# Expert weights split ahead through a DRAM scratch, the last scores first, token halves alternating

## The chip, the cores and the metric

The kernel runs on one core of a Trainium2 chip. A core has five engines with queues of their own: TensorE (PE) multiplies, VectorE (DVE) and ScalarE (ACT) work element by element, GpSimd (POOL) computes a little and issues indirect DMAs, and SyncE (SP) only issues DMAs. They meet at semaphores. The metric is the time of one execution on the device, in microseconds; the median of the runs shown is quoted, and one further execution is profiled.

## The reference, cut to what matters

N = 4096 tokens, D = 512 features, E = 8 experts.

```python
# graph attention, with a residual
q = layernorm(x) @ Wq.T + bq;  k = key @ Wk.T + bk;  v = value @ Wv.T + bv
s = (q @ k.T) / 64 * adj
s = where(abs(s) < 1e-5, -1e9, s)
x = x + (softmax(s) @ v) @ Wm.T + bm
# mixture of experts, two of eight, with a residual
xn   = layernorm(x)
gate = softmax(xn @ Wg + bg);  the top 2 kept and scaled to sum 1
x    = x + sum_e gate_e * (xn @ We[e].T + be[e])
```

## The kernel before

Every large product is made of half-precision parts: an operand is split into a high half (f16) and what is left of it (f16), and three matmuls are summed, high·high, high·low, low·high. `product` does it.

**Folding and projection (until 239 us).** The weights of q and k are folded into one matrix, and those of v and the output projection into another. Keys, values and q are brought into that form by groups of 512 tokens. Keys and values stay in SBUF (`key_region`, `val_region`); q goes to a DRAM scratch, `q_scratch`.

**Attention (32 tiles of 128 query rows; `attend` on each engine, `attend_io` on SyncE).** A tile has 8 chunks of 512 keys. TensorE makes the scores of a chunk (`scores`, 12 matmuls of 128x512) and, one tile behind, the product of a chunk of probabilities with the values (`times_values`, also 12). VectorE multiplies scores with the adjacency (`times_adj`, L967), masks them and finds maxima (`mask`, L974 and L977), ScalarE takes magnitudes (`absolute`, L737) and exponentials (`exponent`, L745 and L750), VectorE splits these (`low_half`, L989), and SyncE turns them with DMA transposes (`turn_probs`, L474). Two tiles behind, the finished rows are normalised and routed: top 2 of 8 experts (`route_top2`), the gates (`route_gates`, for which ScalarE computes one exponential, `gap_exponent`, L784), and the slot that each row gets in its expert's region (`route_slots`, L1089). GpSimd then scatters the rows with two indirect DMAs (`scatter_row`) into a DRAM table `slots`, one table for each half of the tokens. The inverse deviation of the rows (`inverse_deviation`, L618) stands behind these scatters in GpSimd's queue. The single buffer of q, `q_in`, is reloaded at a tile's end (L503), behind the adjacency loads (L465).

Every engine works off its own instructions in the order written. The order within a tile is written out by hand in `attend` and `attend_io`.

**Experts (78 blocks of 128 slots, 39 for each half).** When all rows of a half are in their regions, `tables` computes which rows and which expert each block has. For each block SyncE loads 128 token rows (`load_block`, L547), TensorE turns them (`turn_block`, L1430) and multiplies them with the expert's weights (`multiply_block`, 12 matmuls), ScalarE and VectorE split the turned rows (`block_hi`, `block_lo`), VectorE adds the bias (`block_bias`, L1240), ScalarE applies the gate (`block_gate`, L822), and GpSimd adds the rows to the output with an indirect DMA (`add_block`, L662). If an expert's first block comes up, the accumulations before it must have landed, since the same token may be in both. TensorE turns blocks two ahead of the one that it multiplies. The rest of a region's last block is filled with rows of zero weight (`pad_regions`, 8 DMAs of which each reads its address from a table).

The raw expert weights are loaded in 1 MB pieces over the keys' space and next to it once the last scores are done (L527, L532, L796); ScalarE and VectorE split them, half an expert at a time (`expert_hi`, L798; `expert_lo`, L1197), the first eight halves beside the last tile's probabilities and the other eight between the first eight blocks. Blocks of the first half all come before those of the second.

Of the kernel before, what the change touches and what calls it, by code (L numbers as in the profile page):

```python
# [6 lines left out]
F16 = mybir.dt.float16  # L7
# [12 lines left out]
def graph_attention_moe_kernel(nc, x, adj, keyT, valueT, Wq, bq, Wk, bk, Wv, bv, WmT, bm, Wg, bg, WeT, be, outs):  # L20
# [37 lines left out]
    EARLY = 23  # L58
    LATE = 7
# [8 lines left out]
    assert TURN % RING == 0 and (BLOCKS - EARLY) % TURN == 0 and (BLOCKS - LATE) % TURN == 0 and (T % HALVES) == 0  # L68

    SPLIT_EARLY = C  # L70
    assert SPLIT_EARLY == E and 2 * E - SPLIT_EARLY <= EARLY
# [7 lines left out]
    with ctx:  # L79
# [15 lines left out]
        we = key_region[:, :].rearrange("p (h e k o) -> p h e k o", h=2, e=E, k=KC)  # L95
# [43 lines left out]
        q_in1 = q1_words.bitcast(F16).rearrange("p (h k n) -> p h k n", h=2, k=KC)  # L139
        behind = q1_words[0:1, 0:BLOCKS * E].rearrange("p (b e) -> p b e", b=BLOCKS)  # L140
# [4 lines left out]
        we_odd = carve(KC * D).rearrange("p (k o) -> p k o", k=KC)  # L145
        tokT = carve(YB * KC * P).bitcast(F16).rearrange("p (b h k n) -> p b h k n", b=YB, h=2, k=KC)
        we_even = carve(KC * D).rearrange("p (k o) -> p k o", k=KC)
        we_in = (we_even, we_odd)
# [6 lines left out]
        tok_in += [moe_words[:, at:at + ROW] for at in range(RING * D, RING * D + (RING - YB) * ROW, ROW)]  # L155
        assert len(tok_in) == RING and 12288 + YB * ROW <= 14848
# [73 lines left out]
        o_bank = ps[:, 4, :]  # L230

# [15 lines left out]
        weT_v = WeT.rearrange("e (k p) o -> e p k o", p=P)  # L247
# [61 lines left out]
        we_loaded = [sem(f"we_loaded{b}") for b in range(2)]  # L309
        we_hi = sem("we_hi")  # L310
        we_lo = sem("we_lo")
        be_loaded = sem("be_loaded")
# [24 lines left out]
        tok_loaded = [sem(f"tok_loaded{b}") for b in range(RING)]  # L337
# [9 lines left out]
        halves_of_k = (slice(0, KC // 2), slice(KC // 2, KC))  # L347
# [3 lines left out]
        class Step:  # L351


            def __init__(self, first, turn, h):
                self.first, self.turn, self.h = first, turn, h
                self.at = first + turn * TURN if not is0(turn) else first
                self.b2, self.bank, self.b8, self.meta = first % 2, first % YB, first % RING, first % TURN
# [13 lines left out]
            def has(self, back):  # L371
                return self.first >= back

        def early_steps():
            return [Step(s, 0, 0) for s in range(EARLY)]

        def late_steps():
            return [Step(BLOCKS + s, 0, 1) for s in range(LATE)]

        def turn_steps(j, h):  # L380

            return [Step((EARLY, BLOCKS + LATE)[h] + i, j, h) for i in range(TURN)]

        TURNS = ((BLOCKS - EARLY) // TURN, (BLOCKS - LATE) // TURN)

        AHEAD = 2
        MIDDLE = (SEQ - EARLY) // TURN

        def middle_steps(j):

            return [Step(EARLY + i, j, None) for i in range(TURN)]

        def end_steps():
            return [Step(s, 0, None) for s in range(EARLY + MIDDLE * TURN, SEQ)]

        def ahead(st):

            return Step(st.first + AHEAD, st.turn, None)
# [4 lines left out]
        def _(sp):  # L403
# [77 lines left out]

            def attend_io(t, h=None, last=False):

                turn_probs(t - 1, 0)
# [20 lines left out]
            def pad_regions(h):  # L505
# [997 lines left out]
```

## Time and profile before

| | us |
|---|---|
| median of 3 runs | 1904.28 (1902.39 to 1905.7) |
| the profiled execution | 1899.79 |
| its span, first to last instruction | 1898.1 |
| TensorE busy | 1817.8 (96%) |
| VectorE, ScalarE, GpSimd busy | 1176.2, 730.1, 239.4 |
| granted clock of TensorE, mean | 0.981 of full speed |

The page's row of slices has TensorE at 9 tenths or more until slice 33 of 40, and holes in slices 34 to 37. A row of the stages view gives, for a stretch in us from the span's start, its length, then for PE, PEld (weight loads), DVE, ACT and POOL the busy time with the number of instructions in brackets, and at the end the granted clock, the busy share of the 16 DMA engines, and GB/s. A row of a timeline gives start, duration, engine, line, operation, output and inputs, and in square brackets how long the engine had been idle before it and for what. SPq and ACTq are the issues of DMAs; the duration there is that of the issue. The chain of waits is the chain of work that ended last, with start and duration of each link.

### The profile page before, as it was taken

The numbers are of one execution on the slowest core, as the hardware profiler recorded it, in microseconds if no ns is written. First come the engines' busy times: TensorE is split into PE (matmuls) and PEld (weight loads), VectorE is DVE, ScalarE is ACT, GpSimd is POOL, SyncE is SP. The second block draws the span as 40 slices with busy tenths as digits, with TensorE's granted clock in tenths as the row PEclk, the third lists the DMA queues.
The fourth block names the chain that finished last, engine by engine and source line by source line (L and its number), as shares of the span: only waits on it lengthen the run. The fifth ranks groups of instructions, "written<-read, shape, count | busy, mean of one in ns | idle before, by whom it ended". The sixth has DMA issues, their size and how long they took to land.

```text
span 1898.1 us, 32739 instructions
## 1 busy us (share of the span) xinstructions
PE 1817.8 (96%) x8730; PEld 851.0 (45%) x8731; DVE 1176.2 (62%) x3056; ACT 730.1 (38%) x1381; POOL 239.4 (13%) x277
## 2 busy tenths in 40 slices
PE   8999999999999999999999999999999996789994
PEld 4544444444444444444444444444444443345552
DVE  2788766666666666666666666666666664634542
ACT  1444444443333344433333344433333442433341
POOL 1000000100000000000000000000000010444454
PEclk9999999999999999999999999999999998899997
DMA  5355455555555555555556555555555558788785
GB/s 200 111 177 188 172 136 124 140 142 137 139 138 133 133 133 145 137 142 134 139 128 176 135 135 144 134 145 133 138 133 136 134 137 244 180 194 165 162 161 78
DMA packets 410860, 279.67 MB, mean 147 GB/s; under 512 B 316737, under 2 KB 316737, under 8 KB 410690
## 3 DMA queue, kind: packets, MB, share of 16 engines
q1 hardware_dynamic: 390914, 234.55, 47.8%
q0 software_dynamic: 16736, 38.35, 10.2%
q10 hardware_dynamic: 3168, 6.29, 1.0%
q8 instruction: 16, 0.26, 0.1%
q14 instruction: 26, 0.21, 0.0%
HBM read 144.29 MB, written 59.33 MB: 107 GB/s over the span
## 4 chain that ended last, share of the span: by engine, by line
PE 75%; DVE 8%; DMA 7%; issue 5%; SPq 2%; ACT 2%; DVEq 0%; POOLq 0%; POOL 0%; ACTq 0%
PE ps L1280 16%; PE ps L1282 16%; PE ps L1281 16%; PE ps L1380 8%; PE ps L1381 8%; PE ps L1382 8%; DMA work<-q_scratch 4%; DVE work L967 2%; PE ps L1289 2%; PE ps L1430 1%; ACT work L737 1%; DMA work<-in_WeT 1%; DMA work<-work 1%; PE ps L1327 1%; DVE work L974 1%
## 5 line engine op out<-in xcount | busy, mean ns | idle before, releaser
L1280 PE MATMUL ps<-key_region,work 128*128 128x512 f16 (+1 forms) x1336 | 509.9, 382 | 9.8 <-DMA work<-q_scratch 7.0
L1281 PE MATMUL ps<-key_region,work 128*128 128x512 f16 (+1 forms) x1336 | 509.4, 381 | 0.0
L1282 PE MATMUL ps<-key_region,work 128*128 128x512 f16 (+1 forms) x1336 | 509.2, 381 | 0.0
L1380 PE MATMUL ps<-val_region,work 128*128 128x512 f16 x1024 | 389.6, 380 | 16.3 <-DMA work<-work 11.4
L737 ACT ACTIVATE work<-work 128x512 f32<-128x512 f32 x256 | 161.3, 630 | 597.2 <-DVE work L967 597.1
L1382 PE MATMUL ps<-val_region,work 128*128 128x512 f16 x1024 | 389.6, 380 | 0.0
L1381 PE MATMUL ps<-val_region,work 128*128 128x512 f16 x1024 | 389.5, 380 | 0.0
L967 DVE SCALAR_TENSOR_TENSOR work<-ps,r_cur,work 128x512 f32<-128x512 f32 x256 | 191.8, 749 | 179.0 <-PE ps L1282 163.3
L989 DVE TENSOR_TENSOR work<-work 128x512 f16<-128x512 f32 x256 | 176.4, 689 | 84.0 <-ACT work L750 83.1
L977 DVE CUSTOM_DVE_ANT_0 work<-work 128x512 f32<-128x512 f32 x256 | 177.3, 693 | 51.2 <-DVE work L974 51.0
L1280 PEld LDWEIGHTS ps<-key_region,work 128*128 128x128 f16 x1336 | 131.2, 98 | 172.9 <-issue 28.8
L745 ACT ACTIVATE work<-work,exp_bias 128x512 f32<-128x512 f32 x256 | 181.4, 708 | 65.6 <-DVE exp_bias L985 61.5
L1282 PEld LDWEIGHTS ps<-key_region,work 128*128 128x128 f16 x1336 | 131.4, 98 | 158.8 <-issue 3.4
L1281 PEld LDWEIGHTS ps<-key_region,work 128*128 128x128 f16 x1336 | 131.3, 98 | 148.0 <-issue 3.0
L750 ACT ACTIVATE work<-work,exp_bias 128x512 f16<-128x512 f32 x256 | 180.7, 706 | 0.0
L974 DVE TENSOR_SCALAR work<-work 128x512 f32<-128x512 f32 x256 | 109.2, 426 | 113.2 <-ACT work L737 109.2
L1380 PEld LDWEIGHTS ps<-val_region,work 128*128 128x128 f16 x1024 | 100.2, 98 | 131.8 <-DMA work<-work 12.0
L1382 PEld LDWEIGHTS ps<-val_region,work 128*128 128x128 f16 x1024 | 100.4, 98 | 122.0 <-issue 1.9
L1381 PEld LDWEIGHTS ps<-val_region,work 128*128 128x128 f16 x1024 | 100.4, 98 | 114.0 <-issue 1.5
L662 POOL DMA_INDIRECT out<-val_region,tok_ids x78 | 123.9, 1588 | 152.7 <-DMA out<-val_region,tok_ids 66.6
L627 POOL COPY work<-gate 128x1 f32<-128x1 f32 x64 | 14.6, 228 | 856.9 <-DVE slots_u L1089 776.6
L822 ACT ACTIVATE val_region<-work,tok_gates 128x512 f32<-128x512 f32 x78 | 56.3, 722 | 160.6 <-DVE work L1240 138.8
(149 smaller groups left out, 1542.9 us busy)
## 6 DMA issues: line engine op xcount, KB each, us to landing
work<-in_adj SPq DMA_DIRECT2D x256, 256.0 KB, 2.8
work<-slots SPq DMA_DIRECT2D x40, 257.0 KB
val_region<-slots SPq DMA_DIRECT2D x38, 257.0 KB
work<-in_valueT SPq DMA_DIRECT2D x8, 1024.0 KB, 6.8
work<-in_x SPq DMA_DIRECT2D x8, 1024.0 KB, 5.0
work<-in_keyT SPq DMA_DIRECT2D x8, 1024.0 KB, 5.4
q_scratch<-work SPq DMA_DIRECT2D x8, 1024.0 KB, 5.0
work<-q_scratch SPq DMA_DIRECT2D x32, 256.0 KB, 3.0
```

Of the source, the lines that this page charges most:

```text
L737: nc.scalar.activation(w[:, c * CW:(c + 1) * CW], s_adj[:, c % 2, :], ACT.Abs).then_inc(abs_done, 1)
L745: nc.scalar.activation(prob[:, c % 2, :], w[:, c * CW:(c + 1) * CW], ACT.Exp, bias=exp_bias[:, :], scale=1.0 / SS, accum_out=sum_part[:, c ...
L750: nc.scalar.activation(p_split[:, c, 0:CW], w[:, c * CW:(c + 1) * CW], ACT.Exp, bias=exp_bias[:, :], scale=1.0 / SS).then_inc(p_hi, 1)
L967: nc.vector.scalar_tensor_tensor(s_adj[:, c % 2, :], s_bank(c), r_cur[:, :], adj_in[:, c % ADJ, :], ALU.add, ALU.mult).then_inc(s_read, 1)
L977: nc.vector.tensor_tensor_reduce(out=masked, in0=s_adj[:, c % 2, :], in1=masked, scale=1.0, scalar=-3.0e38, op0=ALU.add, op1=ALU.max, accu ...
L989: nc.vector.tensor_tensor(p_split[:, c, CW:2 * CW], prob[:, c % 2, :], p_split[:, c, 0:CW], ALU.subtract).then_inc(p_lo, 1)
L1280: nc.tensor.matmul(bank, st[0], mv[0], start=(k == 0), stop=False)
L1281: nc.tensor.matmul(bank, st[0], mv[1], start=False, stop=False)
L1282: last = nc.tensor.matmul(bank, st[1], mv[0], start=False, stop=(k == n - 1))
L1380: nc.tensor.matmul(o_bank, st[0], mv[0], start=first, stop=False)
L1381: nc.tensor.matmul(o_bank, st[0], mv[1], start=False, stop=False)
L1382: last = nc.tensor.matmul(o_bank, st[1], mv[0], start=False, stop=final)
```

## The change

Weights. In attention tiles 2 to 17 (the first half), each half of an expert is loaded in four pieces of 256 columns, split by ScalarE and VectorE, and stored as f16 halves in a DRAM scratch, `we_halves`. After the last scores ScalarE issues the loads of expert 0 from the scratch; those of experts 1 to 7, with each expert's bias row, once the last probabilities have been turned. SyncE passes their arrival on through one semaphore, `we_ready`. The splitting at the end is gone.

Last tile. TensorE makes the scores of the last tile before most of the value products of the tile before (`attend_last`). The last tile's values are summed in another PSUM bank.

Blocks. 15 blocks of the first half lead, then 48 blocks alternate between the halves, then 15 of the second half are the tail. Token buffers are 16 instead of 8. The second half's padding is issued by ScalarE after block 9; its last rows are scattered behind accumulations 6 and 8.

```diff
-    EARLY = 23
-    LATE = 7
+    LEAD = 15
+    TOKS = 16
+    PIECES = 4
+    WP = D // 2
+        we_stage = q1_words[:, 0:WP]
+        we_halves = q1_words[:, WP:2 * WP].bitcast(F16).rearrange("p (h o) -> p h o", h=2)
+        o_last = ps[:, 3, :]
+        weT_parts = WeT.rearrange("e (a k p) (c o) -> (e a) p k c o", a=2, p=P, c=2)
+        we_dram = nc.dram_tensor("we_halves", (2 * E, P, 2, 2 * D), F16, kind="Internal").ap()
...
 # SyncE
+            def split_piece(i, q):
+                if not (is0(i) and q == 0):
+                    sp.wait_ge(piece_lo, i * PIECES + q)
+                settle()
+                sp.dma_start(we_stage, weT_parts[i, :, q // 2, q % 2, :]).then_inc(piece_loaded, 16)
+            def store_piece(i, q):
+                sp.wait_ge(piece_lo, i * PIECES + q + 1)
+                settle()
+                sp.dma_start(we_dram[i, :, :, q * WP:(q + 1) * WP], we_halves).then_inc(piece_stored, 16)
             def attend_io(t, h=None, last=False):
+                splits = h == 0
+                if splits:
+                    split_piece(t - 2, 0)
                 turn_probs(t - 1, 0)
...
                 turn_probs(t - 1, 3)
+                if splits:
+                    store_piece(t - 2, 0)
+                    split_piece(t - 2, 1)
                 if h is not None:
                     residual_io(t - 2, h)
                 adjacency(t, 7)
                 for c in range(ADJ, C):
                     turn_probs(t - 1, c)
                     if not last:
                         adjacency(t + 1, c - ADJ)
                     if c == 4 and h is not None:
                         turn_rows(t - 2)
+                    if splits and c in (5, 6, 7):
+                        store_piece(t - 2, c - 4)
+                        if c < 7:
+                            split_piece(t - 2, c - 3)
                 if not last:
                     sp.wait_ge(s_mm, t * C + C)
                     settle()
                     sp.dma_start(q_in, q_dram[t + 1]).then_inc(q_loaded, 16)
...
+            def expert_ready(e):
+                sp.wait_ge(we_loaded[e], 48)
+                sp.sem_inc(we_ready, 1)
+            for st in lead[:YB]:
                 load_block(st)
+            expert_ready(0)
+            sp.wait_ge(pv_mm, T * C)
+            load_block(lead[4])
+            load_block(lead[5])
+            sp.wait_ge(x1_done, T)
+            sp.dma_start(out_tiles[1][TH - 1], x1_out).then_inc(x1_stored, 16)
+            expert_ready(1)
+            turn_rows(T - 1)
+            for st in lead[6:]:
+                load_block(st)
+            for e in range(2, E):
+                expert_ready(e)
+            sp.wait_ge(slotted, 32 * T)
+            sp.wait_ge(padded[1], 16 * E)
+            (48 blocks of turn_steps, 15 of tail_steps)
...
 # ScalarE
+            def piece_high(i, q):
+                act.wait_ge(piece_loaded, i * (PIECES * 16) + (q + 1) * 16)
+                if not (is0(i) and q == 0):
+                    act.wait_ge(piece_stored, i * (PIECES * 16) + q * 16)
+                nc.scalar.activation(we_halves[:, 0, :], we_stage, ACT.Copy, scale=WS).then_inc(piece_hi, 1)
                 for c in range(2, 4):
                     absolute(t, c)
+                    if splits:
+                        piece_high(t - 2, c - 2)
                 if routes:
                     split_rows(t - 2)
                 for c in range(4, 7):
                     absolute(t, c)
+                    if splits and c > 4:
+                        piece_high(t - 2, c - 3)
                 if routes:
                     gap_exponent(t - 2)
                 absolute(t, 7)
...
+            act.wait_ge(piece_stored, 16 * PIECES * 2 * E)
+            act.wait_ge(s_mm, T * C)
+            load_expert(0)
             for c in range(C):
                 exponent(T - 1, c)
-                if c >= 4:
-                    expert_hi(c - 4)
...
+            for b in range(PTR):
+                act.wait_ge(pT_loaded[b], 16 * 2 * T)
+            for e in range(1, E):
+                load_expert(e)
+                load_bias(e)
...
+                if st.first == 9:
+                    act.wait_ge(tables_done, 2)
+                    for e in range(E):
+                        at = act.value_load(pad_at[0:1, 1, e:e + 1], min_val=0, max_val=(DUMMY - 1) * P)
+                        nc.scalar.dma_start(slots[1][bass.ds(at, P), :], pad_row[:, :]).then_inc(padded[1], 16)
...
 # VectorE
+            def piece_low(i, q):
+                dve.wait_ge(piece_hi, i * PIECES + q + 1)
+                nc.vector.scalar_tensor_tensor(we_halves[:, 1, :], we_stage, WS, we_halves[:, 0, :],
+                                               ALU.mult, ALU.subtract).then_inc(piece_lo, 1)
                 times_adj(t, 3)
+                piece_low(t - 2, 0)          # each only in tiles 2 to 17
                 mask(t, 3)
...
                 mask(t, 4)
+                piece_low(t - 2, 1)
                 times_adj(t, 5)
                 mask(t, 5)
+                piece_low(t - 2, 2)
                 times_adj(t, 6)
                 mask(t, 6)
                 route_top2(t - 2)
                 route_gates(t - 2)
+                piece_low(t - 2, 3)
                 times_adj(t, 7)
...
+            dve.wait_ge(piece_stored, 16 * PIECES * 2 * E)
             tables(0)
...
 # TensorE
+            def attend_last():
+                t = T - 1
+                scores(t, 0)
+                scores(t, 1)
+                for c in range(C - LAG, C):
+                    times_values(t - 2, c)
+                for c in range(2, 6):
+                    scores(t, c)
+                times_values(t - 1, 0)
+                scores(t, 6)
+                times_values(t - 1, 1)
+                gate_logits(t - 2)
+                scores(t, 7)
+                for c in range(2, C):
+                    times_values(t - 1, c)
+                    if c == 4:
+                        ranks(t - 2)
```

## Rows read from the trace of the kernel before

**Rows 1.** Stages view: attention tiles 13 to 25, and a free stretch of blocks.
```profile
800.00:1300.00 500.00, 493.99 (x2385) 223.59 (x2384) 322.77 (x893) 191.81 (x395) 35.50 (x57) 1.00 0.57 140
1700.00:1750.00 50.00, 50.00 (x264) 26.98 (x263) 23.37 (x63) 19.27 (x32) 20.08 (x14) 1.00 0.86 188
```

**Rows 2.** Waits of TensorE until 1540 us, then three links of the chain.
```profile
PE ps L1280 <- DMA work<-q_scratch: 7.0, 23, 0.5
...
580.83 2.95 DMA work<-q_scratch
...
622.88 3.04 DMA work<-q_scratch
...
1510.62 3.17 DMA work<-q_scratch
```

**Rows 3.** Timelines of one attention tile: PE, SP, DVE, ACT.
```profile
541.86 0.39 PE L1280 MATMUL ps<-key_region,work 128*128 128x512 f16 x1 [0.17 <-DMA work<-q_scratch]
...
568.96 0.34 SPq L465 DMA_DIRECT2D work<-in_adj  x1
...
574.13 0.33 SPq L465 DMA_DIRECT2D work<-in_adj  x1
...
580.17 0.34 SPq L465 DMA_DIRECT2D work<-in_adj  x1
...
573.15 0.75 DVE L967 SCALAR_TENSOR_TENSOR work<-ps,r_cur,work 128x512 f32<-128x512 f32 x1 [2.33 <-PE ps L1282]
...
577.84 0.15 DVE L1071 TENSOR_SCALAR den<-egap 128x1 f32<-128x1 f32 x1 [0.35 <-ACT egap L784]
...
578.82 0.17 DVE L1077 TENSOR_TENSOR picked<-pick 128x8 f16<-128x8 f32 x1
579.19 0.75 DVE L967 SCALAR_TENSOR_TENSOR work<-ps,r_cur,work 128x512 f32<-128x512 f32 x1 [0.20 <-DVE picked L1077]
...
577.53 0.20 ACT L784 ACTIVATE egap<-gap 128x1 f32<-128x1 f32 x1 [2.89 <-DVE gap L1065]
```

**Rows 4.** Adjacency loads (page; line's view), a copy of a piece, its subtraction.
```profile
work<-in_adj SPq DMA_DIRECT2D x256, 256.0 KB, 2.8
...
DMA to landing us min/median/max: 2.6/2.8/4.0
...
1561.15 1.04 ACT L798 ACTIVATE key_region<-work 128x1024 f16<-128x1024 f32 x1
...
L1197 DVE SCALAR_TENSOR_TENSOR key_region<-work,key_region x16: 1215/1224/1226, 1564.4 to 1644.2; 128x1024 f16<-128x1024 f32 x16
...
  ACT key_region L798: 15.6, 8
```

**Rows 5.** TensorE's clock after waits: its timeline, then the stages view.
```profile
1562.78 0.38 PE L1380 MATMUL ps<-val_region,work 128*128 128x512 f16 x1 [1.82 <-DVE work L1009]
...
1576.27 0.39 PE L1380 MATMUL ps<-val_region,work 128*128 128x512 f16 x1 [2.97 <-DMA work<-work]
...
1577.60:1580.60 3.00, 2.99 (x15) 1.22 (x13) 2.25 (x6) 0.23 (x1) 0.00 (x0) 0.50 1.17 386
...
980.00:985.00 5.00, 3.29 (x16) 1.55 (x17) 3.60 (x10) 0.63 (x1) 0.57 (x1) 1.00 0.87 209
```

**Rows 6.** Timelines of the last tile and the first blocks: PE, DVE, POOL, SP.
```profile
1589.05 0.61 PE L1380 MATMUL ps<-val_region,work 128*128 128x512 f16 x1 [8.46 <-DMA work<-work]
...
1601.52 0.39 PE L1280 MATMUL ps<-key_region,work 128*128 x1 [0.41 <-issue]
...
1617.08 1.09 PE L1430 MATMUL ps<-ident,val_region 128*128 128x128 f32 x4 [5.33 <-DVE work L1232]
...
1658.99 0.68 PE L1430 MATMUL ps<-ident,val_region 128*128 128x128 f32 x4 [2.83 <-DVE work L1232]
...
1598.02 0.17 DVE L1089 CAST slots_u<-slots_f 128x2 uint32<-128x2 f32 x1
...
1610.39 0.57 POOL L618 TENSOR_TENSOR rstd<-var_eps,neg_half 128x1 f32<-128x1 f32 x1 [2.19 <-DMA slots<-work,slots_u]
...
1681.56 11.26 SPq L511 DMA_DIRECT2D slots<-pad_row  x8
```

More of the change, by code:

```diff
@@ L307, in graph_attention_moe_kernel @@
         x1_stored = sem("x1_stored")
[L309 to L312, printed above, removed]
+        piece_loaded = sem("piece_loaded")
+        piece_hi = sem("piece_hi")
+        piece_lo = sem("piece_lo")
+        piece_stored = sem("piece_stored")
+        we_loaded = [sem(f"we_loaded{e}") for e in range(E)]
+        we_ready = sem("we_ready")
         pads_ready = sem("pads_ready")
@@ L351, in graph_attention_moe_kernel, with __init__ @@
         class Step:
[L354 to L357, printed above, removed]
+            def __init__(self, first, turn=0, later=False):
+                self.first, self.turn, self.later = first, turn, later
+                middle = LEAD <= first < SEQ - LEAD
+                self.h = (first - LEAD) % 2 if middle else int(first >= LEAD)
+                if middle:
+                    k = (first - LEAD) // 2 + (0 if self.h else LEAD)
+                else:
+                    k = first if first < LEAD else first - BLOCKS
+                at = k + self.h * BLOCKS
+                self.at = at if is0(turn) else at + turn * (TURN // 2)
+                self.b2, self.bank, self.b8, self.b16 = first % 2, first % YB, first % RING, first % TOKS
             def count(self, back=0):
@@ L371, in has, with ahead, lead_steps, turn_steps @@
             def has(self, back):
[L372 to L398, printed above, removed]
+                return self.later or self.first >= back
+            def ahead(self):
+                return Step(self.first + AHEAD, self.turn)
+        def lead_steps():
+            return [Step(s) for s in range(LEAD)]
+        def turn_steps(j, later=False):
+            return [Step(LEAD + i, j, later) for i in range(TURN)]
+        def tail_steps():
+            return [Step(s) for s in range(SEQ - LEAD, SEQ)]
+        TURNS = (SEQ - 2 * LEAD) // TURN
         block = ctx.enter_context(nc.Block())
@@ L1373, in times_values @@
                 pe.wait_ge(pT_loaded[c % PTR], t * 16 * (C // PTR) + 16 * (c // PTR + 1))
-                if c == 0 and not is0(t):
+                if c == 0 and isl(t, T):
+                    pe.wait_ge(s_read, T * C)
+                elif c == 0 and not is0(t):
                     pe.wait_ge(x1_done, t)
+                bank = o_last if isl(t, T) else o_bank
                 for m in range(MT):
@@ L1379, in times_values @@
                     first, final = c == 0 and m == 0, c == C - 1 and m == MT - 1
-                    nc.tensor.matmul(o_bank, st[0], mv[0], start=first, stop=False)
-                    nc.tensor.matmul(o_bank, st[0], mv[1], start=False, stop=False)
-                    last = nc.tensor.matmul(o_bank, st[1], mv[0], start=False, stop=final)
+                    nc.tensor.matmul(bank, st[0], mv[0], start=first, stop=False)
+                    nc.tensor.matmul(bank, st[0], mv[1], start=False, stop=False)
+                    last = nc.tensor.matmul(bank, st[1], mv[0], start=False, stop=final)
                 last.then_inc(pv_mm, 1)
```

250 lines of the change are left out of this document (105 added, 145 removed).

## The prediction

> **What bounds the kernel now.** I read the stages first. In the attention stretch TensorE is busy 494 of 500 us at full clock, and in the expert stretch 50 of 50 us [rows 1]. Between them and behind them are the holes: TensorE waits 8.46 us for a transposed tile and 5.33 us for VectorE [rows 6]. Time is to be had in the last 340 us, and there is almost none to give in the 32 attention tiles before. Then I asked what those tiles wait for. TensorE waits 23 times for `work<-q_scratch`, 7.0 us in all [rows 2], and a tile starts on it 0.17 us late [rows 3]. So the reload of q, issued last in each tile, is on the path already, with no slack. On SyncE it stands 0.66 us behind the last adjacency load (580.17 [rows 3], 580.83 [rows 2]), which itself follows the last score product of VectorE, 579.19 + 0.75 [rows 3]. A tile takes 622.88 − 580.83 = 42.05 us [rows 2]. Whatever delays that product, or is put between it and the reload, lengthens the tile one for one.
>
> **The change, part by part.**
>
> *Eight pieces of traffic in each of 16 attention tiles.* Tiles 2 to 17 get four pieces each: a 128 KB load, a scaled copy on ScalarE, a subtraction on VectorE, a 128 KB store. There is one staging buffer, so load q+1 waits until the subtraction of q is done, and the copy of q+1 waits for load q+1 and for store q. ScalarE and VectorE are in order, and behind these copies stand operations of the routing.
> Prices: the copy of 1024 columns takes 1.04 us and the subtraction 1.22 us [rows 4], and the 128x512 ones on the same engines some 0.63 and 0.75; for 256 columns I take 0.39 and 0.40. A load lands at best 2.6 us after issue (2.8 median, 256 KB) [rows 4]. Half the bytes can take off a little and the company of a store can add a little; I take 2.6, with 1.7 and 3.4 as ends. An issue behind another costs SyncE 0.66 us.
>
> Walk one tile (q landed at 541.86, times of rows 3):
> 1. Pieces 0 and 1. Piece 0's load is issued in SyncE's idle time at the tile's start. Store 0 and load 1 push residual loads and the last adjacency load by some 2.5 us; the next user is 10 us off. ScalarE waits in copy 1 until load 1 lands, about 563, and the row split behind it comes some 2 us later, still before VectorE wants it. Price nothing; the cover is VectorE's own waits for TensorE, 1 to 2 us a chunk.
> 2. Piece 2. SyncE reaches store 1 and load 2 only behind the adjacency load of 568.96. Load 2 is issued at 568.96 + 2x0.66 = 570.28, lands at 572.9; copy to 573.3, subtraction to 573.75. The product for chunk 6, which ran at 573.15, stands behind it: 0.6 us late.
> 3. Piece 3. The next adjacency load waits for that product: 574.13 + 0.6. Then store 2 and load 3: 574.73 + 1.32 = 576.05, landed 578.65, copied 579.05. On ScalarE the exponent of the gate gap stands behind the copy: it ran at 577.53, now at 579.05, 1.5 us late. VectorE waits for it (its den, 577.84), finishes the picks (578.82), and then has subtraction 3 to do, 0.40, ahead of the last score product (579.19). That product is 1.9 us late.
> 4. Store 3 stands before the reload of q: 0.66 more. Sum 1.5 + 0.4 + 0.66 = 2.56; I take 2.5 us a tile, and 16 x 2.5 = 40 us.
> Nothing absorbs it: the walk starts from products that are pinned to TensorE (573.15 waits for its matmuls), so each tile repeats it. If piece 3 were never late, 0.40 + 0.66 = 1.06 would stay, 17 us in all. With a landing of 3.4 us the two loads add 1.6: 4.1, 66 us.
>
> The Trainium skill ("DMA: Bandwidth & Descriptors", Latency and other measured facts) puts the fixed cost of a DMA at about 2 us, dominated by the receipt. By an estimate from that page, 128 KB at its 358 GB/s limit would land in 2.4 us, and the walk would give 2.2 us a tile, 35 us. No row here has a load of this size.
>
> *The clock.* TensorE's gap per tile grows from about 0.5 to 3.0 us. A wait of 2.97 us was followed by a stretch of 3.0 us at 0.50, the 1.2 GHz level; a wait of 1.82 us was not, nor was the stretch with a 3 us gap at 980 (clock 1.00 all through) [rows 5]. Each fall costs at least half of 3.0, 1.5 us. Between none and all 16 tiles (0 to 24 us) I take six: 9 us.
>
> *VectorE's wait for the last store before the first tables.* It comes once, and the tables already delay a tile; the store lands about when q does. 1 us, between 0 and 3.
>
> *Last scores first.* The final chunk is scored two value chunks earlier (2 x 12 x 0.216 = 5.2 us), and the raw weights (now only expert 0's, before the softmax) no longer share the DMA engines with the last transposes, which is where I put the 8.46 us wait. The last tile's accumulator moves to its own bank, so the 1.82 us wait for VectorE goes too. Removed: 1.82 + 2.97 + 8.46 = 13.3 us of waits, and half of the 8.2 us at clock 0.50 between them (3.0 and 5.2, one row shown), 4.1 us. Late next: chunk 3 to 5 of the last scores wait for VectorE, 0.4, and a transpose 0.5. Gain 16.5 us, between 10 and 18.
>
> *Weights for experts 1 to 7.* 21 DMAs, 8.75 MB, are issued on ScalarE's queue when the last transpose has landed. At 0.4 us each ScalarE is held 8 to 9 us before it can copy the first token block; this lies beside GpSimd's chain from slots_u (1598.02) to the deviation (1610.39), which sets VectorE's and TensorE's 5.33 us wait anyway [rows 6], and that wait stays. But GpSimd's two scatters in this chain now share the DMA engines with all the weights at once: 3 us, between 0 and 8. The Trainium skill (same page, "Issuing engines are not separate DMA queues") says that transfers from all issuing engines interleave on the same 16 DMA engines, so another queue saves issue time only. By that rule this term is not zero; the trace agrees, in the 8.46 us that TensorE waited for a transpose while raw weights came in [rows 6].
>
> *Splitting gone from the blocks.* The blocks multiplied behind the transposes of 1617.08 and before those of 1658.99 are eight, 3 to 10: 41.9 us [rows 6]. A split stands in each of the first, and VectorE waited 15.6 us for ScalarE's halves [rows 4]. At the pace of the free stretch, 264 matmuls in 50 us, or 16 a block and 3.03 us [rows 1], they are worth 24.2. Of the 17.7 us, the tables and top-2 of the last tile keep about 5. Gain 12.5, between 6 and 15.
>
> *Pads of the second half.* Eight DMAs with register loads took SyncE 11.26 us [rows 6], and the token loads behind them stopped TensorE, for about as long. Now ScalarE issues them after block 9, with the copies of the token blocks behind them; TensorE is two blocks (6 us) ahead, and the first loads of the middle wait for them too. I cost the new stall like the old, 11 to 12 us: nothing, between 4 lost and 8 gained.
>
> *Ring of 16, alternating halves, other register arithmetic, bias loads by expert.* Token loads are not what the free stretch waits for, and the count of expert changes and dummy blocks, at which GpSimd waits for earlier accumulations, stays: nothing. The cover is GpSimd's slack; without it each of some 20 changes would cost about 1 us.
>
> Sum: 40 + 9 + 1 − 16.5 + 3 − 12.5 = +24 us. The profiled execution took 1899.79 us (span 1898.1 and 1.7 around it), so it becomes 1924; the median of the runs is 4.5 higher, so 1904.3 + 24 = **1928**.
>
> **Rivals.**
> 1. *The pieces are hidden, the kernel gets faster.* If load 3 lands within 1.7 us of 575.45 (574.13 + 1.32), the exponent is on time, and only 17 us are lost, with the gap too short for the clock: 17 + 1 − 26 = −8, **1896**. For it: the transfers are small and the DMA engines idle there. Against it: the fastest of 252 adjacency loads took 2.6.
> 2. *The tail gives all it has.* From 1617 to the span's end at 1898 are 281 us; the 75 blocks left are worth 227 at the free pace, and the drain behind TensorE some 27. That is 27 less, with 16.5 in front 43 in all. 50 − 43 = +7, **1911**.
> 3. *The clock falls in nearly every tile and landings are slow.* 54 + 24 − 26 + 1 = +53, **1957**. For: 2.97 us was enough once.
> 4. *The tail's traffic takes its gain back.* Gain 10 instead of 26: **1944**. For: 8.75 MB in a burst, DMA share already near full in the expert stretch [rows 1]. This is the case in which the change doesn't do what it says.
>
> **Chances.** Forecast 0.40; rival 1 0.19, rival 2 0.16, rival 3 0.13, rival 4 0.12. The range 1889 to 1957 leaves a tenth at either end. No change means within 0.2% (3.8 us), about what the runs can tell. Faster 0.24 (rival 1, a third of rival 2), same 0.07, slower 0.69.
>
> **What would show it.** In the profile after: tile period 44.5 instead of 42.0 us in tiles 2 to 17 and unchanged behind; `q_scratch` as the wait of TensorE with 2 to 3 us each; the gap exponent behind the piece copy with an idle time put down to the piece load; a clock of 0.50 after some tile starts; first block product 12 to 16 us nearer to the last tile's start (now 1601.52 − 1513.79 = 87.7 [rows 2, 6]); blocks at 3.0 us with one hole near block 12. Wrong if the period of tiles 2 to 17 stays below 43.2 us, or if the stretch from the last tile's start to the end (1898.1 − 1513.8 = 384 us now) shortens by over 35 us.

## The result, and the profile after

| | before | after |
|---|---|---|
| median of 4 runs, us | 1904.03 (1902.39 to 1905.7) | 1959.75 (1956.37 to 1962.13) |
| the profiled execution, its span | 1899.79, 1898.1 | 1956.37, 1954.4 |
| start of the last attention tile (q landed) | 1513.8 | 1582.2 |
| from there to the end of the span | 384.3 | 372.2 |
| granted clock, mean | 0.981 | 0.976 |

The change makes the kernel slower: ratio 1.0291, 95% interval 1.027 to 1.0313. That is 55.7 us, where I forecast 24 and a range to 1957. The sign and the split into a loop that loses and a tail that gains were right. Both sizes were wrong: the loop loses 68.4 us (1582.2 − 1513.8; forecast 50 with the clock and the tables' wait), and the tail gains 12.1 (forecast 26). The period of tiles 2 to 17, from one start to the next, is 46.55 us on average (333.75 to 1032.02, 15 periods), where the forecast had 44.5; behind them it is 42.1 as before.

The waits of TensorE until 1600 us, profile after (total us, times, longest), which answer to [rows 2]:
```profile
PE ps L1319 <- DMA work<-q_scratch: 56.6, 27, 3.6
...
PE ps L1439 <- DVE picked L1118: 2.2, 7, 0.4
```
The reload of q is late by 56.6 us in all instead of 7.0: 49.6 us more in 16 tiles, 3.1 us each. The page of the profile lists what its chain of waits runs through:
```profile
PE ps L1319 14%; PE ps L1321 14%; PE ps L1320 14%; PE ps L1422 6%; PE ps L1423 6%; PE ps L1424 6%; DMA work<-in_WeT 4%; DMA work<-q_scratch 4%; DMA out<-val_region,tok_ids 3%; DVE work L1008 3%; SPq L494 2%; PE ps L1328 1%; SPq L466 1%; PE 
```
Two transfers of the new pieces are on the path: their loads (`in_WeT`, 4%) and their stores (`SPq L494`, 2%). The chain of waits at one tile's end (start, us, what):
```profile
596.73 0.34 SPq L466
597.40 0.59 SPq L494
598.25 2.68 DMA work<-in_WeT
600.95 0.43 ACT work L785
601.52 0.22 issue
601.75 0.76 DVE work L1008
602.84 0.35 SPq L466
603.53 0.59 SPq L494
604.39 2.87 DMA work<-in_WeT
608.62 0.24 DVE pick L1117
609.51 0.75 DVE work L1008
610.49 0.34 SPq L466
611.16 0.59 SPq L494
612.08 2.94 DMA work<-q_scratch
```
This is the walk of the prediction, link by link: adjacency load, store 1, load 2, its copy, the score product of chunk 6 behind the subtraction; adjacency load, store 2, load 3, the picks, the last product, adjacency load, store 3, q. ScalarE's and VectorE's timelines show the two holdings:
```profile
600.95 0.42 ACT L785 ACTIVATE work<-work 128x256 f16<-128x256 f32 x1 [3.72 <-DMA work<-in_WeT]
...
607.28 0.42 ACT L785 ACTIVATE work<-work 128x256 f16<-128x256 f32 x1 [4.05 <-DMA work<-in_WeT]
607.60 0.19 ACT L818 ACTIVATE egap<-gap 128x1 f32<-128x1 f32 x1
```
```profile
601.40 0.42 DVE L1185 SCALAR_TENSOR_TENSOR work<-work 128x256 f16<-128x256 f32 x1 [2.81 <-ACT work L785]
...
607.90 0.15 DVE L1112 TENSOR_SCALAR den<-egap 128x1 f32<-128x1 f32 x1 [1.81 <-ACT egap L818]
```
The exponent of the gate gap stands directly behind the copy that waited for its load. The next tile then begins so (TensorE's timeline, with the idle time in brackets), and the stages view of what follows has the clock at 0.51, the lower level (1.2 GHz):
```profile
615.15 0.39 PE L1319 MATMUL ps<-key_region,work 128*128 128x512 f16 x1 [3.23 <-DMA work<-q_scratch]
...
616.40 0.63 PE L1321 MATMUL ps<-key_region,work 128*128 128x512 f16 x1
```
```profile
616.00:619.00 3.00, 3.00 (x9) 1.03 (x8) 1.01 (x3) 2.16 (x6) 0.18 (x1) 0.51 0.90 210
```
There are ten such stretches between 333 and 1036 us: nine of 8 matmuls and one, the first, of 14. Matmuls that start 0.43 us apart instead of 0.22 cost 0.21 each, 86 of them 18 us. With 49.6 that is 67.6 of the 68.4 us.

In the tail, ScalarE's timeline of the weight and bias issues (first, longest and last group, and the first copy of a token block):
```profile
1644.87 1.22 ACTq L828 DMA_DIRECT2D key_region<-we_halves  x2
...
1657.72 4.31 ACTq L832 DMA_DIRECT2D work<-in_be  x1
...
1667.68 1.12 ACTq L832 DMA_DIRECT2D work<-in_be  x1
1668.86 1.08 ACT L854 ACTIVATE work<-ps 128x512 f16<-128x512 f32 x2 [24.55 <-issue]
```
and behind it VectorE, TensorE and GpSimd, each in its timeline:
```profile
1669.49 0.69 DVE L1273 TENSOR_TENSOR work<-ps,work 128x512 f16<-128x512 f32 x1 [20.11 <-ACT work L854]
```
```profile
1670.32 1.08 PE L1493 MATMUL ps<-ident,work 128*128 128x128 f32 x4 [14.90 <-DVE work L1273]
...
1706.91 0.63 PE L1493 MATMUL ps<-ident,val_region 128*128 128x128 f32 x4 [2.57 <-DVE work L1273]
...
1721.76 1.09 PE L1493 MATMUL ps<-ident,val_region 128*128 128x128 f32 x4 [5.87 <-DVE work L1273]
```
```profile
1673.00 0.57 POOL L645 TENSOR_TENSOR rstd<-var_eps,neg_half 128x1 f32<-128x1 f32 x1 [13.46 <-DVE var_eps L1066]
```
Twenty-one issues hold ScalarE for 24 us. The first block waits for it, and so does the last tile's routing, which stands behind `block_lo` on VectorE: GpSimd's deviation waits 13.46 us for VectorE, where before it waited 2.19 for its own scatter [rows 6].

The same timelines split the tail into three stretches. The first block's product comes 89.3 us after the start of the last tile (before 87.7): 1.6 us lost. From there to the end of the last block's product it is 253.7 us (before 269.2): 15.5 gained. What is left behind TensorE is 29.2 us (before 27.3): 1.9 lost.

### The profile page after: what moved, and what is told of

Read it like the earlier page. It is cut to its first block, busy times and chain, and to the rows that moved or that the text cites. A ratio compares the mean times of both kernels' runs of the same rounds, so it can differ in the third digit from the quotient of the medians.

```text
span 1954.4 us, 33715 instructions
## 1 busy us (share of the span) xinstructions
PE 1828.6 (94%) x8730; PEld 851.7 (44%) x8731; DVE 1179.9 (60%) x3104; ACT 735.9 (38%) x1429; POOL 235.9 (12%) x277
## 4 chain that ended last, share of the span: by engine, by line
PE 65%; DMA 13%; DVE 7%; issue 6%; SPq 4%; ACT 2%; ACTq 2%; POOLq 1%; DVEq 0%; POOL 0%
PE ps L1319 14%; PE ps L1321 14%; PE ps L1320 14%; PE ps L1422 6%; PE ps L1423 6%; PE ps L1424 6%; DMA work<-in_WeT 4%; DMA work<-q_scratch 4%; DMA out<-val_region,tok_ids 3%; DVE work L1008 3%; SPq L494 2%; PE ps L1328 1%; SPq L466 1%; PE ps L1493 1%; PE ps L1366 1%
## 5 line engine op out<-in xcount | busy, mean ns | idle before, releaser
L1319 PE MATMUL ps<-key_region,work 128*128 128x512 f16 (+1 forms) x1336 | 515.9, 386 | 59.3 <-DMA work<-q_scratch 56.6
L1321 PE MATMUL ps<-key_region,work 128*128 128x512 f16 (+1 forms) x1336 | 515.1, 386 | 0.0
L1320 PE MATMUL ps<-key_region,work 128*128 128x512 f16 (+1 forms) x1336 | 515.0, 385 | 0.0
L1273 DVE TENSOR_TENSOR work<-ps,work 128x512 f16<-128x512 f32 x78 | 53.8, 690 | 113.4 <-ACT work L854 113.4
```

The source lines that it names most:

```text
L1319: nc.tensor.matmul(bank, st[0], mv[0], start=(k == 0), stop=False)
L1320: nc.tensor.matmul(bank, st[0], mv[1], start=False, stop=False)
L1321: last = nc.tensor.matmul(bank, st[1], mv[0], start=False, stop=(k == n - 1))
```

## The experiments

My theory A was the walk of the prediction, mis-sized. The rival B: the pieces cost by their traffic, wherever they are placed, by competing with the transposes and adjacency loads for the 16 DMA engines. For the tail, A: ScalarE's issues hold back the blocks; the rivals are named in the expectations. Each batch was timed beside the kernel before (medians 1905.76, 1906.61, 1907.34); ratios are against it. That median was 1904.03 when the changed kernel was timed, so times of different batches can't be told apart to better than some 3 us.

**1. The changed kernel without the pieces.**
```diff
-                splits = h == 0
+                splits = False
-    ... we_dram[2 * e + a]).then_inc(we_loaded[e], 16)
+    ... q_dram[4 * e + 2 * a:4 * e + 2 * a + 2] ...
```
This kernel leaves out the expert weights: its tail loads parts of q of the same size in their place. It also has no wait for the last store before the tables.


> The kernel after the change without the pieces in tiles 2 to 17 (no loads, copies, subtractions, stores); the tail is untouched, its weights are loaded from the q scratch in the same descriptors, so the expert weights are left out of the result. Theory A (the pieces cost the attention tiles all of the 68 us by which the last tile starts late): last tile starts at about 1514, time 1892, give or take 3. Rival B (part of the 68 us is something else in the new program, such as the split loops or the wait before the tables): time over 1900.


Measured 1890.22 (1887.94 to 1892.49), ratio 0.9919, interval 0.9895 to 0.9944. The pieces cost 69.5 us (1959.75 − 1890.22), more than the whole loss, and all else together gains 15.5. q's reload is back at a wait of 6.9 us in all.

**2. Store 3 behind the reload of q.**
```diff
-                    if splits and c in (5, 6, 7):
+                    if splits and c in (5, 6):
...
                     sp.dma_start(q_in, q_dram[t + 1]).then_inc(q_loaded, 16)
+                if splits:
+                    store_piece(t - 2, 3)
```


> The kernel after the change with one edit: store 3 of each tile is issued behind the reload of q. Theory A (what stands before the reload of q in SyncE's queue lengthens the tile one for one): 0.85 to 1.0 us less a tile, 14 to 16 us, and some falls of the clock fewer, 0 to 10 us: 1933 to 1946. Rival B (the reload is late because the DMA engines carry more traffic, whatever the order): within 3 us of 1960.


Measured 1939.76 (1938.25 to 1941.26), ratio 1.0179, interval 1.0156 to 1.0202: 20 us for one store moved by one place. TensorE's wait for q falls by 13.6 us:
```profile
PE ps L1321 <- DMA work<-q_scratch: 43.0, 25, 2.8
```
That is 0.85 us a tile, about what a store takes on SyncE in the chain above (0.85 to 0.92 from its issue to the next). The rest is clock. With gaps of 2.2 to 2.8 us at the tile starts it falls behind two of them (556.52 and 737.14) instead of ten. A third fall, near 1026 us, comes with another wait, for VectorE in the tile that computes the tables, which is 4.4 us long here and 0.6 in the changed kernel:
```profile
1026.51 0.58 PE L1424 MATMUL ps<-val_region,work 128*128 128x512 f16 x1 [4.40 <-DVE work L1052]
```
About 29 matmuls run at the lower level instead of 86, which is 12 us; 13.6 and 12 less the 3.8 us of this longer wait come to 22, near the 20 measured.

**3. Twelve matmuls of no use at the end of tiles 2 to 17.** They fill TensorE's gap and shorten nothing.
```diff
+                for _ in range(fill):
+                    nc.tensor.matmul(ps[:, 7, :], kT[:, 0, 0, 0:P], kT[:, 0, 0, 0:CW], start=True, stop=True)
```


> The kernel after the change with 12 further matmuls of 128x512 at the end of tiles 2 to 17, into a PSUM bank that nothing reads there; at 0.216 us each they take 2.6 us of TensorE's wait for q, which is over 3 us. Theory A (the clock fell in 10 of these tiles for 3.4 us each and cost 1.7 us each time, because TensorE idled): no falls between 340 and 1030 us, 17 us less, 1943. Rival C (the falls cost nothing, since the chain through SyncE sets the tile anyway): within 3 us of 1960. Rival D (the fill comes in the way of the next scores): over 1965.


Measured 1945.73 (1944.72 to 1946.73), ratio 1.0211, interval 1.0189 to 1.0233: 14 us back. The stages view has the clock at full speed where the changed kernel had 0.98 (first row experiment 3, then the changed kernel):
```profile
300.00:800.00 500.00, 489.64 (x2351) 219.94 (x2350) 312.23 (x857) 196.52 (x418) 35.19 (x55) 1.00 0.61 150
```
```profile
300.00:800.00 500.00, 461.38 (x2168) 204.98 (x2167) 303.65 (x842) 186.63 (x398) 32.42 (x53) 0.98 0.60 146
```
One fall is left, at 1034 us, behind a wait of 2.31 us for VectorE. So the clock's share of the loss is at least 14 us, and it goes with TensorE's idle time: the same waits, filled, bring no fall.

**4. The same pieces, placed early.** Loads 1, 2 and 3 and the stores go 10 to 15 us earlier on SyncE, and the copies and subtractions with them, and the last store stands ahead of the last adjacency load but one. Every transfer and every operation of the change is kept.
```diff
                 adjacency(t, 5)
+                if splits:
+                    store_piece(t - 2, 0)
+                    split_piece(t - 2, 1)
                 turn_probs(t - 1, 2)
...
-                    store_piece(t - 2, 0)
-                    split_piece(t - 2, 1)
+                    store_piece(t - 2, 1)
+                    split_piece(t - 2, 2)
...
                     turn_probs(t - 1, c)
+                    if splits and c == 6:
+                        store_piece(t - 2, 3)
...
+                    if splits and c == 4:
+                        store_piece(t - 2, 2)
+                        split_piece(t - 2, 3)
-                    if splits and c in (5, 6, 7):
-                        ...
```


> The kernel after the change with the same four pieces a tile, same sizes and engines, at other places: every piece is loaded 6 to 10 us before its copy, piece 3 is subtracted before chunk 6, and nothing of a piece stands between the row split and the gap exponent or between the last adjacency load and the reload of q. Theory A (it is the order behind in-order queues, not the work): tile period back to 42.0 to 42.4, last tile starts at 1514 to 1520, time 1892 to 1899. Rival B (the traffic and the work of the pieces cost the tile time wherever they stand): 1925 to 1960.


Measured 1892.36 (1889.51 to 1896.66), ratio 0.9926, interval 0.9905 to 0.9946: faster than before, and within 2.2 us of the kernel without any pieces. The reload of q has nearly its old period again, 42.39 us between the two links shown and 42.16 on average over 15 tiles (before 42.10), and the gate gap's exponent has its old wait, for VectorE:
```profile
497.02 3.28 DMA work<-q_scratch
539.41 3.00 DMA work<-q_scratch
```
```profile
578.22 0.20 ACT L826 ACTIVATE egap<-gap 128x1 f32<-128x1 f32 x1 [2.89 <-DVE gap L1114]
```
The edit is less than the expectation says: copies 2 and 3 still stand between the row split and the gate gap's exponent, and load 3 is still young, so that ScalarE waits for it once a tile, 15.6 us in all instead of 170.8. Neither makes the exponent late. This settles the loop. The traffic and the arithmetic of the pieces cost some 2 us; their place costs 67 us. B is refuted.

**5. Experiment 4, with experts 2 to 7 issued one by one behind the gates of blocks 0 to 5.**
```diff
-            for e in range(1, E):
-                load_expert(e)
-                load_bias(e)
+            load_expert(1)
+            load_bias(1)
...
                 block_gate(st)
+                if st.first + 2 < E:
+                    load_expert(st.first + 2)
+                    load_bias(st.first + 2)
```


> The kernel with the early pieces, and the weights of experts 2 to 7 issued by ScalarE one expert at a time behind the gates of blocks 0 to 5, instead of all in a row ahead of the first token block. Theory A (the 21 issues hold ScalarE for 24 us, since the queue fills, and the first token block waits for that): the first block product some 15 us earlier against the last tile's start (89 us now), the fourth (block 3) 10 to 14 earlier; 8 to 14 us less than with the early pieces alone (1892): 1878 to 1884. Rival B (GpSimd's chain from the slots to the deviation, slowed by the weights' traffic, sets the blocks anyway): within 3 us of 1892.


Measured 1888.15 (1886.06 to 1890.11), ratio 0.9907, interval 0.9889 to 0.9924. A wait of 14.1 us at the first block is gone, and 4 us came of it, between the two expectations; the intervals of experiments 4 and 5 overlap.

**6. Experiment 4, with the pads of the second half issued by SyncE.**
```diff
-                if st.first == 9:
-                    (ScalarE: wait for the tables, 8 pads)
...
 # SyncE
+            sp.wait_ge(tables_done, 2)
+            (8 pads)
             sp.wait_ge(slotted, 32 * T)
             sp.wait_ge(padded[1], 16 * E)
```


> The kernel with the early pieces, and the pads of the second half issued by SyncE (behind the first 15 token loads) instead of by ScalarE. Theory A (ScalarE's 9.1 us of issues keep it from the next token block, TensorE stands 5.9 us and falls to 1.2 GHz for a while): 5 to 8 us less than 1892, 1884 to 1887. Rival B (the first loads of the middle wait for the same pads, so the hole stays, it only gets another name): within 3 us of 1892.


Measured 1891.74 (1889.11 to 1894.78), ratio 0.9934, interval 0.9913 to 0.9955: no difference from experiment 4. The hole near block 12 is only renamed; TensorE now waits there for the token loads:
```profile
1660.50 1.11 PE L1500 MATMUL ps<-ident,val_region 128*128 128x128 f32 x4 [11.49 <-DMA val_region<-slots]
```

**7. Experiment 6, with the blocks in the order of before** (all of the first half's, then the second's, as `EARLY = 23`, `LATE = 7` had them).
```diff
-    LEAD = 15
+    LEAD = 23
+    LATE = 7
...
-                middle = LEAD <= first < SEQ - LEAD
-                (halves by turns in the middle)
+                self.h = int(first >= BLOCKS)
+                self.at = first if is0(turn) else first + turn * TURN
```


> As e6_pads_sp, and the blocks in the order of the kernel before: all 39 of the first half, then the second. Theory A (alternating needs the second half's pads by block 15, in sequence they are needed by block 39): the hole near block 12 to 15 goes, 0 to 4 us less than e6_pads_sp, 1880 to 1887. Rival B (alternating halves saves GpSimd waits between accumulations that TensorE feels): 3 us or more above e6_pads_sp.


Measured 1882.44 (1880.26 to 1886.21), ratio 0.9887, interval 0.9869 to 0.9905: 9.3 us less than experiment 6, where 0 to 4 were expected, and that hole is gone. Alternating brings the second half's first block, and with it the wait for its tables and pads, to block 15 instead of block 39; in sequence they are done by then. But sequence alone is not the reason: the kernel before has it too, and has a hole of this size at its pads (TensorE's timeline, before):
```profile
1697.40 1.11 PE L1430 MATMUL ps<-ident,val_region 128*128 128x128 f32 x4 [9.05 <-DMA val_region<-slots]
```
Experiment 7 has 16 token buffers instead of 8 and issues the pads at 1640 instead of 1682 us. Which of these it takes was not tried.

**8. The kernel before, with the last scores first alone.**
```diff
-            with pe.Fori(2, T) as t:
+            with pe.Fori(2, T - 1) as t:
                 attend(t, True)
+            attend_last()
```


> The kernel before with the last tile's scores first on TensorE and nothing else; raw weights are still loaded and split at the end. Theory A (the waits of 13 us before the blocks are transposes that share the DMA engines with raw weights; the order alone gives only the 4 us by which the last softmax is earlier): 0 to 5 us less than before, 1900 to 1905. Rival B (the order is what frees them): 12 us or more less, 1892 or below.


Measured 1905.33 (1900.77 to 1907.94), ratio 0.9997, interval 0.9981 to 1.0012: nothing. TensorE still waits for its transposes, and for the tail behind them (first two rows of its timeline; they answer to 2.97 and 8.46 in [rows 5, 6]):
```profile
1576.26 0.39 PE L1380 MATMUL ps<-val_region,work 128*128 128x512 f16 x1 [3.71 <-DMA work<-work]
...
1588.08 0.61 PE L1380 MATMUL ps<-val_region,work 128*128 128x512 f16 x1 [7.19 <-DMA work<-work]
```
The order alone doesn't remove them. In the changed kernel, where the raw weights are gone as well, TensorE is busy throughout that stretch:
```profile
1582.20:1640.00 57.80, 57.76 (x277) 26.39 (x278) 36.19 (x93) 26.62 (x57) 5.98 (x9) 1.00 0.63 143
```
The forecast put those waits down to the raw weights' traffic. That is not shown: besides the traffic, the changed kernel has no splits beside the last probabilities and another bank for the last tile's values, and the three were not tried apart.

**9. Everything that helped: experiment 7 with experiment 5's spread.**
```diff
+    (experiment 7's edits)
             load_expert(1)
             load_bias(1)
+    (experiment 5's edit)
```


> Three edits of the tail and the early pieces together: pieces placed early, pads issued by SyncE, blocks in the order of the kernel before, and experts 2 to 7 issued one per block behind gates 0 to 5. Theory A (ScalarE's long row of issues holds back the first blocks): the sequence alone gave 1882.4 with a first wait of 13.6 us for the deviations and gates; the spread took 4 us of it in the kernel with alternating halves, so 1874 to 1880 here. Theory B (the first blocks are bound by GpSimd's chain or by the weights' own landing, the issues only stand in front of it): within 3 us of 1882, 1879 to 1885.


Measured 1880.46 (1879.36 to 1883.64), ratio 0.9864, interval 0.9847 to 0.9882: the fastest version, but only 2 us under experiment 7, and their runs overlap. That lies in B's range, and just above A's.

**10. The changed kernel with the spread alone.**
```diff
                 block_gate(st)
+                if st.first + 2 < E:
+                    load_expert(st.first + 2)
+                    load_bias(st.first + 2)
```


> The changed kernel as it is, with one edit: experts 2 to 7 issued one per block behind gates 0 to 5 instead of all in a row ahead of the first block. Theory A (the row of issues costs the same whatever the loop does): 4 us off the changed kernel's 1959.8, 1953 to 1958, and TensorE's first long wait of the tail falls from 14.9 to under 5 us. Theory B (the changed kernel's tail starts from a later and fuller ScalarE, so the row costs the whole of its 24 us less the 9 forecast): 15 us off, 1942 to 1948.


Measured 1960.01 (1959.54 to 1962.14), ratio 1.0278, interval 1.026 to 1.0297: nothing. The wait of 14.90 us ahead of the first product is gone and the longest wait in the first eight blocks is 4.47, as theory A had it, but no time came of it; both theories missed on the time. TensorE's timeline has the first and the ninth product (the last row is the changed kernel's ninth):
```profile
1660.31 0.38 PE L1321 MATMUL ps<-key_region,work 128*128 x1
...
1673.59 1.09 PE L1495 MATMUL ps<-ident,val_region 128*128 128x128 f32 x4 [4.47 <-DVE work L1275]
...
1701.46 0.39 PE L1321 MATMUL ps<-key_region,work 128*128 x1 [0.34 <-DVE work L1283]
```
```profile
1698.57 0.38 PE L1319 MATMUL ps<-key_region,work 128*128 x1
```
The first product comes 11 us earlier, although this execution entered its last tile 4.9 us later (1587.1 against 1582.2): 16.1 us nearer to the start of that tile. At the ninth product 2.1 are left of these 16 us (114.3 against 116.4). They are lost where the issues now stand: ScalarE has six groups of three, 15 us in all, between its copies of the first token blocks, and between 1669 and 1699 us the chain of waits runs through three of the groups (issues from it):
```profile
1690.82 0.73 ACTq L828
1691.59 2.36 ACTq L832
...
1697.64 0.63 ACTq L828
```
So I read the edit as one that moves the row of issues and doesn't take it away. The same happens from experiment 4 to 5 (the first product 16.1 us nearer, the ninth 4.7) and from 7 to 9 (13.8 and 1.5). What the tail is worth without these issues on ScalarE was not tried.

GpSimd is the next bound. Its accumulations (the line's view, experiment 10, then experiment 7):
```profile
L689 POOL DMA_INDIRECT out<-val_region,tok_ids x78: 1541/1542/1636, 1670.7 to 1950.3; - x78
```
```profile
L700 POOL DMA_INDIRECT out<-val_region,tok_ids x78: 1542/1543/1897, 1611.5 to 1871.0; - x78
```
The 78 accumulations take 260 to 280 us in all these versions (276.0 before). At an expert's first block GpSimd waits for the previous accumulation to land (experiment 7, chain of waits, three of its last links):
```profile
1802.07 5.68 DMA out<-val_region,tok_ids
...
1846.02 5.89 DMA out<-val_region,tok_ids
...
1858.56 5.72 DMA out<-val_region,tok_ids
```
In experiment 7 there are 1.85 us from one issue to the next without a wait, and 21 waits of over 3 us that sum to 114. By an estimate from these, GpSimd needs about 114 + 78 x 1.54 + 57 x 0.3 = 251 us, 3.2 us a block, where TensorE needs 3.03 [rows 1]; it is an upper end, since the timeline puts six of the 21 waits down to ScalarE. Between 1680 and 1870 us the chain of waits runs through these landings for 68% of the time in experiment 7 and for 43% in experiment 10, but for 7% in the changed kernel, where TensorE's matmuls have 61%. TensorE is not slowed: from the 21st product to the last it takes 3.01 to 3.05 us a block in all four (experiments 7, 9, 10 and the changed kernel). So GpSimd's chain is what a faster front would meet next, and not what took the 16 us. I did not take its waits away: the kernel has them because the same token may be in both blocks.

## Why the prediction was wrong

Two steps failed in the loop, both in size, and one in the tail, in its overlap: a piece was to delay a tile by 2.5 us and delays it by 3.1; the clock was to fall six times and fell ten times; and ScalarE's row of weight issues was to lie beside GpSimd's chain and stands ahead of it.

**The pieces in the tiles (40 us): mechanism right, mis-sized.** Measured 49.6, 3.1 a tile instead of 2.5. Taken from the same adjacency load to the issue of q, the walk has 14.43 us and the tile shown 15.35 (596.73 to 612.08). The three stores are 0.6 of the difference: I priced every issue at 0.66, the step between two adjacency loads, and a store's own issue is 0.59 with 0.86 to the next (603.53 to 604.39). The two loads on the path took 2.68 and 2.87 instead of 2.6. The median of all 64 is 2.6, so the value for a landing was right. The Trainium skill ("DMA: Bandwidth & Descriptors", Latency and other measured facts) puts the fixed cost of a DMA at about 2 us. The trace agrees roughly: the fastest of the 64 loads took 2.1 us in all, and the median stands above the 2.4 estimated from that page.

**The clock (9 us): half of what it cost.** It fell ten times, not six, and a fall costs 1.7 us, not 1.5 (the first 3): 18 us, of which experiment 3 gave 14 back. I had bounds of 0 and 24 and no row with gaps of 3 us that repeat; six was a guess between them. A gap 0.9 us shorter, in experiment 2, has the clock fall behind two of 16 gaps. So the size of the gap and the clock are one term, and an error of 0.6 us a tile costs twice.

**The tables' wait (1 us):** measured 0.2.

**Last scores first (−16.5): the place is right, the time did not come.** In the changed kernel the first block's product comes at 89.3 us instead of 87.7. In experiment 10, without the row of issues in front, it comes 73.2 us after the last tile's start (1660.31 − 1587.1): 14.5 nearer, in the forecast 12 to 16. Experiment 8 shows that the reordering alone gives none of it.

**The weights for experts 1 to 7 (+3): this step failed.** I wrote that ScalarE "is held 8 to 9 us" and that "this lies beside GpSimd's chain". It is held 24 us, since the issues, priced at 0.4, take 0.55 to 4.31 while the 8.75 MB are landing. And it is not beside the chain but ahead of it: `block_lo` waits for ScalarE, and the last tile's statistics stand behind it on VectorE. I named who waits for ScalarE (TensorE) and did not follow VectorE's queue one step further. With the term before it this was to bring the first product 13.5 us nearer (16.5 − 3), and it is 1.6 further: 15.1 of the miss, more than the 14 by which the whole tail misses. Experiments 5, 9 and 10 move the issues and bring back 4, 2 and nothing, since the issues then stand between the first blocks. That the tail would give the rest with the issues on no engine that the blocks need is argued from the timelines, not shown.

**Splitting gone, alternation, pads (−12.5 and nothing): about right together.** From the first block's product to the last one's end it is 15.5 us less. The pads' hole was costed like the old one, and it is like it: the two blocks there take 16.5 us, before 16.8, where the free pace would be 6.1. It doesn't matter who issues them. The Trainium skill (same page, "Issuing engines are not separate DMA queues") says that another queue saves issue time only; experiment 6 agrees, within a microsecond. Experiment 7 shows that the forecast left something out: without the hole there are 9 us more to be had. "The cover is GpSimd's slack" held for TensorE, whose pace stays at the free one, but the slack is small: GpSimd is 3.5 us behind TensorE at the 21st block of the changed kernel and 21 at the last. Rival 2's 227 us for the last 75 blocks was nearly had in experiment 7: 233.8, from the fourth product on, where the changed kernel has 243.3 and the kernel before 252.6.

**The sum.** 49.6 + 18 + 0.2 − 12.1 = 55.7, against 56.3 between the two spans. The time came out near rival 3's 1957, but partly by luck. Its loop is 79 us (its 54 for the pieces is worked out nowhere; the walk with slow landings has 66) and its tail gains 26; measured are 68.4 and 12.1, two errors that cancel. Its reasons hold for the clock only: the landings were not slow. Rival 4's number for the tail, 10 instead of 26, is close to the measured 12.1. It comes by way of the issues on ScalarE and not of slower transposes; whether the traffic is what makes these issues long was not tried apart.

## What to carry to other kernels

Work that is added to a loop at its bound costs by its place, not by its amount: the same 64 loads, stores, copies and subtractions cost 69 us behind young loads and late stores, and 2 us when they stood 10 to 15 us earlier in the tile. Before adding a load whose user works in the order written, look at what stands behind that user, and let the load be older than its landing time when the engine comes to it. A long row of DMA issues on an engine that others wait for costs in front of their work, and spread between the steps of that work it cost nearly as much here (experiments 5, 9 and 10). And a gain at the front of a pipeline has to be followed to the end: 16 us at the first block were 2 at the ninth.

## What the runs showed of the hardware that I had not expected

- A DMA issue on ScalarE takes 0.40 us when little is in flight, and up to 4.31 us for a bias row of the same kind while the weights are landing (21 issues: 24 us; landings of the weights 4.6 to 13.1 us, median 10.8). With 18 of the 21 spread over the first blocks (experiment 10) their durations sum to 16.8 us instead of 23.0.
- A store from SBUF to DRAM holds SyncE 0.59 us, and a load 0.34 to 0.38.
- A gap of 3.1 to 3.6 us at a tile's start was followed by a clock at half speed in ten of sixteen tiles, and gaps of 2.2 to 2.8 us (experiment 2) in two of sixteen. In the changed kernel's tiles the stretch at half speed was 8 matmuls long in all but the first.
